# Six sweeps over a 5120 x 5120 matrix on one core: turned blocks stored later, x loaded in ten pieces from another queue, TensorE turning the identity at the start

## The reference, cut to what matters

```
x: (5120, 64)   adj A: (5120, 5120)
u = par_u[0]*par_u[1] * (diag_u * x_u) @ W_u + x_u      # first 2048 rows; items the same with W_i
e = concat(u, i)
h = A @ (A.T @ e)                                       # layer 0
x = layernorm(x + layernorm_affine(h) + x)
x = layernorm(x + 1 - 0.1*x - 0.01*sum(x * (A @ x)))     # layer 1
deg = clip(rowsum(A) + 1, 1)
x = layernorm(x + l2norm(relu([x, (A @ x + x)/deg] @ W + b)))   # layer 2
T1 = A @ x;  T2 = 2*A @ T1 - x;  T3 = 2*A @ T2 - T1      # layer 3, four weights
x = layernorm(x + x@w0 + T1@w1 + T2@w2 + T3@w3 + b)
```

## Time and profile before

| | us |
|---|---|
| median of 3 runs | 1547.31 (1545.45 to 1548.04) |
| the profiled execution, its own time | 1544.33 |
| its span, first to last instruction | 1542.5 |
| TensorE busy | 1498.6 (97%) |
| VectorE busy | 599.5 (39%) |
| ScalarE busy | 248.6 (16%) |
| mean granted TensorE clock | 0.992 |
| moved by DMA | 519.07 MB, mean 337 GB/s |

### The profile page before, as it was taken

The page is one execution under the profiler, slowest core; times in us unless marked ns, Lnnn a source line. Parts: engine busy times, 40 slices in busy tenths (PEclk is TensorE's granted clock), DMA queues, the critical chain, the costliest instruction groups (busy, mean ns, idle before and its releaser), DMA issues.

```text
span 1542.5 us, 17449 instructions
## 1 busy us (share of the span) xinstructions
PE 1498.6 (97%) x6598; PEld 704.2 (46%) x6598; DVE 599.5 (39%) x1303; ACT 248.6 (16%) x492; POOL 61.3 (4%) x66
## 2 busy tenths in 40 slices
PE   7899999999999989999999899999999999999898
PEld 5555545555555533334444344444444444444333
DVE  4655555655555477524332443233111021100422
ACT  3333334333343410000100001000000000000000
POOL 0000000000000012100000010010000000000100
PEclk8999999999999999999999999999999999999999
DMA  9999999999999989999787488886488869988896
GB/s 309 408 390 407 409 409 396 390 393 399 386 388 396 337 312 399 421 421 380 296 310 294 164 328 300 298 295 222 141 327 318 304 221 342 337 315 300 342 415 242
DMA packets 122146, 519.07 MB, mean 337 GB/s; under 512 B 20780, under 2 KB 20820, under 8 KB 72020
## 3 DMA queue, kind: packets, MB, share of 16 engines
q1 hardware_dynamic: 105584, 412.68, 72.0%
q10 hardware_dynamic: 16484, 105.31, 16.4%
HBM read 411.79 MB, written 106.17 MB: 336 GB/s over the span
## 4 chain that ended last, share of the span: by engine, by line
issue 99%; POOLq 0%; POOL 0%; DVE 0%
POOL power_out L404 0%; POOLq L402 0%; POOLq L404 0%; DVE rows L854 0%; POOL ident L397 0%; POOLq L399 0%; POOL ident L399 0%; POOLq L1075 0%
## 5 line engine op out<-in xcount | busy, mean ns | idle before, releaser
L689 PE MATMUL ps_u<-blk,vectors 128*128 128x512 f32 (+1 forms) x2000 | 736.7, 596 | 1.4 <-DVE part L1015 1.0
L689 PEld LDWEIGHTS ps_u<-blk,vectors 128*128 128x128 f32 (+1 forms) x2000 | 297.0, 173 | 393.5 <-issue 389.6
L449 ACT ACTIVATE blk<-ps_turn 128x512 f32<-128x512 f32 x400 | 203.2, 605 | 340.2 <-PE ps_turn L526 340.1
L1015 DVE TENSOR_TENSOR part<-part,ps_u 64x512 f32<-64x512 f32 (+1 forms) x45 | 30.4, 685 | 355.1 <-PE ps_u L689 354.5
L555 PE MATMUL ps_h<-blk,u_rows 128*64 128x512 f32 x720 | 164.4, 599 | 0.0
L787 DVE TENSOR_REDUCE row_part<-blk 128x4 f32<-128x2048 f32 x68 | 152.5, 2279 | 1.2 <-DMA blk<-in_adj 0.9
L526 PE MATMUL ps_turn<-ident,blk 128*128 128x128 f32 x1088 | 130.0, 278 | 10.3 <-DMA blk<-in_adj 10.3
L526 PEld LDWEIGHTS ps_turn<-ident,blk 128*128 128x128 f32 x1088 | 121.6, 144 | 30.5 <-issue 25.7
L771 DVE TENSOR_TENSOR part<-part,ps_h 128x512 f32<-128x512 f32 x80 | 55.0, 688 | 189.7 <-PE ps_h L555 189.7
L538 PE MATMUL ps_u<-blk,e 128*64 128x512 f32 x544 | 125.0, 600 | 0.0
L404 POOL TENSOR_TENSOR power_out<-power_in,minus_half 128x4 f32<-128x4 f32 x60 | 60.6, 1010 | 1477.6 <-DVEq L817 1477.6
(11 more groups left out here) (97 smaller groups left out, 601.1 us busy)
## 6 DMA issues: line engine op xcount, KB each, us to landing
blk<-a_transposed SPq DMA_DIRECT2D x291, 1024.0 KB, 6.2
a_transposed<-blk ACTq DMA_DIRECT2D x100, 1024.0 KB, 9.3
blk<-in_adj SPq DMA_DIRECT2D x68, 1024.0 KB, 13.9
nat_far<-in_adj SPq DMA_DIRECT2D x32, 1024.0 KB, 15.3
out<-rows SPq DMA_DIRECT2D x10, 128.0 KB, 4.2
rows<-in_x SPq DMA_DIRECT2D x1, 768.0 KB, 10.1
rows<-in_x SPq DMA_DIRECT2D x1, 512.0 KB, 7.4
w2x<-in_L_gnn_W ACTq DMA_DIRECT2D x4, 16.0 KB, 8.4
```

The lines of the kernel that those rows point to most:

```text
L449: nc.scalar.activation(blk[:, n % RING, t, :], ps_t[t][:, :], ACT.Copy)\
L689: mm = pe.matmul(acc, left, tiles[:, t, :], start=first, stop=last)
L1015: V.tensor_tensor(part[parts, cols], part[parts, cols], ps_both[r % 2][parts, :], ALU.add)\
```

## The change

Three things. (1) `store` is called with n - LATE, LATE = 8: the store of a turned block is issued eight blocks later, and the last eight blocks are stored after the loop. (2) All small inputs and x leave SyncE's queue for ScalarE's. x comes in ten pieces of 128 KB: pieces 0 to 3 up front, pieces 4 to 9 one after each of the first six blocks; each has its own semaphore. (3) TensorE turns the identity 16 times before its first wait for data, and takes `turn_x_in(0)` ahead of `turn_block(0)`. `diag` is turned in another bank, so that VectorE may take it after the first copy; the row sum of block 0 goes between `make_e(0)` and `make_e(1)`.

```diff
+    LATE = 8
...
+        diag_in = ps_u[0][:, 0:NT]
...
-                if n == 0:
-                    sp.dma_start(rows[:, 0:4 * TB, :], x_rows[:, 0:4 * TB, :]).then_inc(x_first_loaded, 16)
-                    sp.dma_start(par[:, 0, :], par_u.partition_broadcast(P)).then_inc(par_loaded, 16)
-                    sp.dma_start(par[:, 1, :], par_i.partition_broadcast(P)).then_inc(par_loaded, 16)
-                if n == 1:
-                    sp.dma_start(rows[:, 4 * TB:NT, :], x_rows[:, 4 * TB:NT, :]).then_inc(x_loaded, 16)
-                    for h in range(2):
-                        sp.dma_start(w0[half(h), 1, :], w_i).then_inc(x_loaded, 16)
...
+            load_x(0)
+            for h in range(2):
+                const(w0[half(h), 0, :], w_u)
             const(diag_flat[0:UT, :], diag_u.rearrange("(t p) -> t p", p=P))
             const(diag_flat[UT:NT, :], diag_i.rearrange("(t p) -> t p", p=P))
-            for h in range(2):
-                const(w0[half(h), 0, :], w_u)
+            const(par[:, 0, :], par_u.partition_broadcast(P), par_loaded)
+            const(par[:, 1, :], par_i.partition_broadcast(P), par_loaded)
+            load_x(1)
             act.wait_ge(ident_ready, 2)
             nc.scalar.activation(first_copy[:, :], ident[:, 0:1], ACT.Copy)
+            load_x(2)
+            load_x(3)
...
-                    if t == 0 and n % 2 == 1:
-                        store(n - 1)
-                if n % 2 == 1:
-                    store(n)
+                    if t == 0 and n % 2 == 1 and n > LATE:
+                        store(n - 1 - LATE)
+                if n % 2 == 1 and n > LATE:
+                    store(n - LATE)
+                if n == 0:
+                    for h in range(2):
+                        const(w0[half(h), 1, :], w_i, w_i_loaded)
+                if 4 + n < NB:
+                    load_x(4 + n)
...
+            for n in range(BLOCKS - LATE, BLOCKS):
+                store(n)
...
             def turn_x_in(i):
-                pe.wait_ge(x_first_loaded, 16)
-                if i > 3:
-                    pe.wait_ge(x_loaded, 16 * N_X_LOADS)
+                pe.wait_ge(x_loaded[i], 16)
...
+            for k in range(16):
+                pe.transpose(ps_t[TB - 1][:, k % TB * P:(k % TB + 1) * P], ident[:, :], ident[:, :])
+            turn_x_in(0)
             turn_block(0)
             turn_diag()
-            turn_x_in(0)
+            times_w(0)
             turn_x_in(1)
-            times_w(0)
             turn_block(1)
             times_w(1)
             turn_x_in(2)
...
             copy_x_in(1)
             make_e(0)
+            sum_rows(0)
             make_e(1)
```

More of the change, by code:

```diff
@@ L146, in build @@
         weights_loaded = sem("weights_loaded")
-        x_first_loaded = sem("x_first_loaded")
-        x_loaded = sem("x_loaded")
+        w_i_loaded = sem("w_i_loaded")
+        x_loaded = [sem(f"x_loaded{i}") for i in range(NB)]
         ident_ready = sem("ident_ready")
@@ L410, in const, with load_x @@
                 act.dma_start(dst, src).then_inc(loaded, 16)
+            def load_x(i):
+                tiles = slice(i * TB, (i + 1) * TB)
+                const(rows[:, tiles, :], x_rows[:, tiles, :], x_loaded[i])
+            load_x(0)
+            for h in range(2):
+                const(w0[half(h), 0, :], w_u)
             const(diag_flat[0:UT, :], diag_u.rearrange("(t p) -> t p", p=P))
             const(diag_flat[UT:NT, :], diag_i.rearrange("(t p) -> t p", p=P))
[L414 to L415 removed]
+            const(par[:, 0, :], par_u.partition_broadcast(P), par_loaded)
+            const(par[:, 1, :], par_i.partition_broadcast(P), par_loaded)
+            load_x(1)
             act.wait_ge(ident_ready, 2)
             nc.scalar.activation(first_copy[:, :], ident[:, 0:1], ACT.Copy)
+            load_x(2)
+            load_x(3)
             def load_rows_of_l0():
@@ L494, in turn_diag @@
                 pe.wait_ge(consts_loaded, 16 * N_CONSTS)
-                pe.matmul(ps_u[1][:, 0:NT], diag_flat[:, :], ident[0:NT, 0:NT], start=True, stop=True)\
+                pe.matmul(diag_in, diag_flat[:, :], ident[0:NT, 0:NT], start=True, stop=True)\
                     .then_inc(diag_turned, 1)
             def turn_x_in(i):
-                pe.wait_ge(x_first_loaded, 16)
-                if i > 3:
-                    pe.wait_ge(x_loaded, 16 * N_X_LOADS)
+                pe.wait_ge(x_loaded[i], 16)
                 if i > 1:
@@ L513, in times_w @@
                     pe.wait_ge(xw_used, i)
+                pe.wait_ge(w_i_loaded if i >= UB else consts_loaded, 32 if i >= UB else 16 * N_CONSTS)
                 for t in range(TB):
@@ L736, in _ @@
             V.tensor_tensor(ident2[:, :], ident[:, 0:F], ident[:, F:P], ALU.add)
[L737 to L743, removed]
             def by_pairs(t):
@@ L789, in _ @@
             copy_x_in(0)
+            dve.wait_ge(par_loaded, 32)
+            V.tensor_tensor(par_prod[:, :], par[:, :, 0], par[:, :, 1], ALU.mult)
+            dve.drain()
+            dve.wait_ge(diag_turned, 1)
+            V.tensor_scalar(diag[:, 0:UT], diag_in[:, 0:UT], par_prod[:, 0:1], None, ALU.mult)
+            V.tensor_scalar(diag[:, UT:NT], diag_in[:, UT:NT], par_prod[:, 1:2], None, ALU.mult)
+            dve.drain()
             copy_x_in(1)
             make_e(0)
+            sum_rows(0)
             make_e(1)
@@ L794, in _ @@
                 later = [i for i in (2 * p + 2, 2 * p + 3) if i < NB]
-                sum_rows(2 * p)
+                if p > 0:
+                    sum_rows(2 * p)
                 for i in later:
```

2 lines of the change are left out of this document (1 added, 1 removed).

## The result

| | before | after |
|---|---|---|
| median of 7 runs each, us | 1548.04 | 1552.98 |
| lowest and highest run | 1545.45, 1550.14 | 1551.38, 1555.63 |
| ratio, with its 95% interval | | 1.0037 (1.0025 to 1.0050) |
| the profiled execution, its own time | 1544.33 | 1552.91 |
| its span | 1542.5 | 1551.1 |

The change makes the kernel slower by 0.37%, or 5.7 us (3.9 to 7.7). The two medians themselves stand 4.9 us apart; the us that I give beside a ratio are always the ratio's. A second profile of before (`e14_before_again`, at the end of the experiments) has a time of 1550.78. So I compare times by the runs, and use the profiles for single stretches.

A forecast was written before the change was run, and what follows sets the result against it. Data bounds the start and the beginning of the row part, TensorE the stretch between. From a median of 1547.31, -3.8 at the start and +9.5 for the drain gave 1553.0, range 1546 to 1558.5.

The forecast's parts named there:

- The identity turns: Before TensorE's first data: 16 turns end before data arrives and win nothing, 1.5 us as the bound.
- The start: First 63 us: without stores and x on SyncE's queue, `u_part(8)` starts at 59.4, a gain of 3.8 us.
- the forecast of piece 3: Start: piece 3 of x, taking turns packet for packet with A, lands at 21.5, so `u_part(0)` starts at 22.
- x comes early: Rival, ScalarE's queue in the first 20 us: piece 3 lands by 14, gain up to 13.0 us; chance 0.15.
- the start wins nothing: Rival at the start: piece 3 at 24 or later behind `par`, time 1557.1, up to 1559; chance 0.08.
- The middle: Steady turning part: stores issued eight blocks later still land before their slots are rewritten, so they cost nothing.
- The drain: Beginning of the row part: eight stores behind the last copy delay load 6 and the loads after it, costing 9.5 us.
- the 7.5 that were the lower bound: End of the turning part: eight stores take 20 us, idle engine time fills 12.5, so at least 7.5 stays.
- The drain is cheaper: Rival at the end: engines pack without a hole, cost 4 instead of 9.5 us, time 1547.5; chance 0.08.
- The sum: Whole kernel: -3.8 at the start and +9.5 at the end make +5.7 us, a median of 1553.0.
- Slots: Rival in the turning part: stores land too late for L446, some us in each pair, over 1560; chance 0.05.
- whether the change does what it says: Rival at the start: SyncE's queue still stalls with six blocks at once; it would not matter, as data flow meanwhile.

The follow-up runs named there:

- e14_before_again: The kernel before, unchanged, run and profiled a second time; 1551.03 us against 1549.76 of before's runs on the same chip, ratio 1.0012.
- e6: The changed kernel without the 16 turns of the identity; 1554.13 us, ratio 1.0032 against before.
- e12: Changed kernel without identity turns, x's first four pieces behind A's first block, store lateness stepped down from block 40; 1537.24 us, ratio 0.9914.
- e1: The kernel before with only the stores eight blocks late, x left on SyncE's queue; 1550.97 us, ratio 1.0017.
- e3: The changed kernel with stores eight blocks late at first, two fewer every 18 blocks, none from block 72; 1548.64 us, ratio 1.0007.
- e8: The changed kernel with the last eight stores issued in reversed order, 99 to 92; 1552.24 us, ratio 1.0020 against before.
- e9: The kernel before with only the last eight stores moved behind the last copy; 1556.08 us, ratio 1.0049.

## Why the prediction was right

**The time.** Forecast 1553.0, measured 1552.98, and the sign comes from the mechanism that was forecast. That the number agrees so closely is luck in part: the profile has a drain 2.3 us larger than forecast, and medians move between sets of runs. The forecast stood on before's 1547.31, which is 1548.04 in the runs beside after.

**The identity turns, 0.** Held (`e6`, `e12`).

**The start, -3.8.** In the profile -3.5; the four executions with this x and late stores (`e6` without identity turns) give 63.5 - 59.5 = 4.0, with single ones from 1.8 to 4.9. The equal packet counts held (1575 to 1577), and with them the forecast of piece 3: landed at 22.3 for 21.5, `u_part(0)` at 23.00 for 22. SyncE issued its first four loads by 3.15 us. After `u_part(0)` it took 36.7 us to `u_part(8)` for the 37.3 forecast. `par` was slow as expected, but it held A's queue back too (59 packets to 58), which the forecast didn't say; no wait for A came of it. Two small flaws of the sum changed nothing: 22 + 37.3 is 59.3 and not 59.4, and no row shows the 0.9 us to land. The rival "x comes early" fell, and "the start wins nothing" fell with it: 23.00 is under 24.4, the bound at which it began, and S is positive.

What the prediction did not see is that this term was itself a sum of two with opposite signs. It priced the stores' absence and the new place of x together; `e1` and the split at `u_part(0)` show the stores' absence to be worth 6.4 to 7.9, of which the new loads gave back 3.4 to 3.9.

**The middle, 0.** Held: M = 480.3 for 480.0, no wait on A. It held for a shift of every store by the same amount. It did not hold for extra stores there (`e3`): "costs nothing as long as it lands in time" is too strong for a stretch that is 94% full.

**The drain, +9.5.** The mechanism was right in each link (stores behind the last copy, slot of block 99 freed late, load 6 late, the run of loads without slack, many small waits ended by block product 57), the size was off: 11.8. In the clock of the last turned block, which comes 3.24 us earlier than before:

- load 6 was issued at 581.68 + 3.24 = 584.9 for 584: 0.9 more;
- it landed 5.0 us after, for 4.8: 0.2 more;
- the 40 loads behind it took 101.3 us to load 46's landing at 688.01, so 2.53 each and not the 2.49 of 421 GB/s: 1.7 more.

9.0 + 0.9 + 0.2 + 1.7 = 11.8. The mis-sized step is the pace of the loads; the prediction had the higher pace only as a bound (2.53 to 2.55 would make it 12; from its 9.0 that comes to 10.6 to 11.4), though the 106.1 us for the same loads before had pointed there, and had taken 0.5 for it. `e8` splits the 11.8 otherwise: 3.0 of hole, 8.8 of volume, and the volume lies above the 7.5 that were the lower bound. `e9`'s 6.3 lies below it, since there only 4.5 MB more fall into the stretch. "The drain is cheaper" fell. The waits on `a_transposed` are 8.1 us, at the lower edge of the 8 to 12 named; before had 0.4 of them, so 4.1 of D are not in waits. About 1.7 are the clock, which is at 1.2 GHz for 6.8 us in this stretch (558 to 565) and for 3.4 before. The other 2.4 are in what the timeline counts as busy: a block product that waits 0.55 starts 2.48 us after the one ahead, one that doesn't 1.72, so each of the 14 waits costs some 0.2 more than it shows.

**The sum.** +5.7 forecast. In the two first profiles it is 8.6; against the mean of before's two profiles at block product 57 (684.8) after is 7.6 later, and the runs say 5.7 (3.9 to 7.7). So a drain 2.3 larger than forecast did not show in the runs, where the profiles' own spread of some us is averaged out; which term the average lowers stays open.

**Slots, and whether the change does what it says.** No wait at the slots of the ring, and the stores come eight blocks later as written.

## What to carry to other kernels

When work is moved out of a crowded place, follow it to where it lands; here the eight stores left a start where they hindered 6 to 8 us and landed in a drain with no slack, where they cost 12. The way out was to move it only for as long as it helps and to pay it back slowly where there is spare, after working out how much spare a block has: here a stretch with a fully busy TensorE and DMA engines at 94% took two extra stores per 24 blocks from block 40 on, and not two per 18 from block 18 on. And a small load that everything waits for is best put near the front of the large loads' own queue: behind the first block of A the first four pieces of x let `u_part(0)` start at 16.5 to 18.6, on the other queue at 22.5 to 23.3. There it got packet for packet with A, so count its packets, not its bytes.

## What the runs showed of the hardware

- Two full queues get the same number of packets whatever the packets hold: 658 to 641 and 1575 to 1577, with 2 KB on one and 256 B on the other, and 59 to 58 in the microsecond in which one had the slow `par`. So 128 KB in 256 B packets took 3.3 us of a full pair of queues: pieces 1, 2 and 3 landed at 15.7, 19.0 and 22.3.
- A broadcast of 8 bytes to 128 partitions slows both queues: the engines moved 107 GB/s from 9 to 10 us in after, and 365 from 7 to 8.
- A gap in TensorE's work is followed by a stretch at 1.2 GHz whose length differs between executions of the same kernel: 3.4 or 6.8 us at the same place, and in the start 11.63 to 28.7 us (`e3`) or 11.77 to 18.6 and 22.01 to 25.43 (after). It holds most of the 6.4 us between two profiles of the same kernel (4.6 of them behind block product 57). How much of the runs' spread up to 1555 comes from it, I haven't measured.
